# Two start-up weight loads move from SyncE's DMA queue to ScalarE's, in an attention plus FFN layer kernel

## The reference

```python
xn = _layernorm(x, axis=-1)
x = x + _L0_attn_ref(xn, Wq, Wk, Wv, Wg, Wo, Ws1, Ws2, bs2, g_norm_weight) \
      + _L0_ffn_ref(xn, gate_W_packed, gate_scales, up_W_packed, up_scales, down_W_packed, down_scales)
```

```python
q = (hs @ Wq.T).reshape(B, T, H, DK)
k = (hs @ Wk.T).reshape(B, T, H, DK)
v = (hs @ Wv.T).reshape(B, T, H, DV).transpose(0, 2, 1, 3)
g = (hs @ Wg.T).reshape(B, T, H, DV)
```

## Time and profile before

| what | value |
|---|---|
| median of 3 runs | 1081.25 us (1080.89 to 1081.56) |
| the profiled execution | 1081.48 us |
| its span | 1079.7 us |
| TensorE busy | 1067.8 us (99%) |
| VectorE busy | 916.1 us (85%) |
| ScalarE busy | 653.8 us (61%) |
| GpSimd busy | 420.4 us (39%) |

### The profile page before, as it was taken

How to read it: one execution, slowest core, us unless ns; L and a number is a source line. 1 busy time by engine, 2 the same in 40 slices (tenths; PEclk the granted TensorE clock), 3 DMA queues, 4 the chain that set the end, 5 groups by cost and what they waited for, 6 DMA issues and landing times.

```text
span 1079.7 us, 20531 instructions
## 1 busy us (share of the span) xinstructions
PE 1067.8 (99%) x7158; PEld 919.4 (85%) x7158; DVE 916.1 (85%) x1679; ACT 653.8 (61%) x2112; POOL 420.4 (39%) x309
## 2 busy tenths in 40 slices
PE   8999999999999999999999999999999999999999
PEld 6788888888888888888888888888888888888888
DVE  6998888888889888889878898889888889888886
ACT  5766665566655576555766556656565665656564
POOL 5353352434523354232643326343253432524332
PEclk9999999999999999999999999999999999999999
DMA  5020000200002000020000200002000010000001
GB/s 172 1 80 2 1 2 1 81 1 1 2 1 81 1 2 1 2 80 2 1 1 1 80 2 2 1 1 81 1 1 1 9 73 1 1 1 2 20 21 40
DMA packets 9558, 23.06 MB, mean 21 GB/s; under 512 B 880, under 2 KB 5872, under 8 KB 8560
## 3 DMA queue, kind: packets, MB, share of 16 engines
q1 hardware_dynamic: 9456, 21.76, 5.6%
HBM read 19.66 MB, written 2.10 MB: 20 GB/s over the span
## 4 chain that ended last, share of the span: by engine, by line
PE 93%; DVE 3%; ACT 1%; issue 1%; DMA 1%; SPq 0%; POOL 0%; DVEq 0%; POOLq 0%; ACTq 0%
PE bank L221 21%; PE bank L223 21%; PE bank L222 21%; PE bank L326 5%; PE bank L396 5%; PE bank L367 3%; PE bank L339 3%; PE bank L328 3%; PE bank L405 3%; PE bank L316 2%; PE bank L342 1%; PE bank L376 1%; PE bank L389 1%; PE bank L358 1%; PE bank L351 1%
## 5 line engine op out<-in xcount | busy, mean ns | idle before, releaser
L1458 POOL TENSOR_TENSOR inter_lo<-ffb,inter_hi 128x512 fp32r<-128x512 f32 x62 | 79.7, 1309 | 446.5 <-ACT inter_hi L811 446.5
L1449 POOL TENSOR_TENSOR qkT<-ra,xs 128x512 f32<-128x512 f32 x128 | 164.8, 1288 | 136.2 <-DVE xs L1121 114.4
L774 ACT ACTIVATE sm<-bank,mx 128x64 f32<-128x64 f32 x256 | 76.5, 325 | 145.3 <-DVE mx L1077 145.2
L1121 DVE TENSOR_TENSOR xs<-xs,rope 128x512 f32<-128x512 f32 x128 | 130.3, 1018 | 0.0
L755 ACT ACTIVATE xs<-bank 64x512 f32<-64x512 f32 x128 | 76.2, 595 | 79.3 <-PE bank L223 48.4
L1118 DVE TENSOR_TENSOR ra<-bank,rope 128x512 f32<-128x512 f32 x128 | 87.9, 687 | 35.2 <-ACT xs L756 33.4
L1066 DVE RECIPROCAL enzT<-enzT 128x256 f32<-128x256 f32 x64 | 111.6, 1744 | 0.0
L221 PE MATMUL bank<-xh,wgu_hi 128*128 128x512 f32 x256 | 105.3, 411 | 0.0
L221 PE MATMUL bank<-xh,wqk_hi 128*128 128x512 f32 x256 | 103.0, 402 | 0.8 <-DVE ffa L1102 0.8
L221 PE MATMUL bank<-wvg_hi,xh 128*128 128x512 f32 x256 | 100.8, 394 | 1.0 <-DVE xl L1177 1.0
L223 PE MATMUL bank<-xh,wgu_lo 128*128 128x512 f32 x256 | 101.0, 395 | 0.0
(11 more groups left out here) (173 smaller groups left out, 3057.0 us busy)
## 6 DMA issues: line engine op xcount, KB each, us to landing
raw<-in_w_qkvg SPq DMA_DIRECT2D x7, 1024.0 KB, 7.2
scaled<-in_w_scaled SPq DMA_DIRECT2D x8, 640.0 KB, 8.3
packed<-in_w_packed SPq DMA_DIRECT2D x8, 384.0 KB, 3.1
acc<-in_x SPq DMA_DIRECT2D x3, 512.0 KB, 9.6
out<-acc SPq DMA_DIRECT2D x3, 512.0 KB, 3.0
raw<-in_w_qkvg SPq DMA_DIRECT2D x2, 512.0 KB, 6.4
acc<-in_x SPq DMA_DIRECT2D x2, 256.0 KB, 3.0
ws_raw<-in_w_slot SPq DMA_DIRECT2D x8, 48.0 KB, 3.0
```

The costliest lines, as they stand in the source:

```text
L774: ins = act.activation(sm[:, c], src[:, c], ACT.Exp, bias=mx[:, g:g + 1], accum_out=ssum[:, g:g + 1])
L1121: dve.tensor_tensor(two(xs[i % 2][:, :]), two(xs[i % 2][:, :]), sin, ALU.mult).then_inc(sin_done, 1)
L1449: pool.tensor_tensor(qkT[:, i, :], ra[i % 2][:, :], xs[i % 2][:, :], ALU.add).then_inc(roped, 1)
L1458: pool.tensor_tensor(dst[1][e], ffb[e][:, :], dst[0][e].bitcast(F32), ALU.subtract).then_inc(inter_lo, 1)
```

## The change

Both weight loads are taken out of SyncE's program and put at the head of ScalarE's, ahead of its first wait. They write the same tiles and raise the same semaphores. SyncE's other loads move up by two places.

```diff
-            first = w_qkvg[0].rearrange("p (k n) -> p k n", k=KT)
             sp.dma_start(acc[:, 0:2, :], x_rows[:, 0:2, :]).then_inc(x_in[0], 16)
             sp.dma_start(acc[:, 2:NT, :], x_rows[:, 2:NT, :]).then_inc(x0_rest_in, 16)
-            sp.dma_start(raw_k[:, :, 512:1024], first[:, :, 512:1024]).then_inc(raw0_in, 16)
-            sp.dma_start(raw_k[:, :, 0:512], first[:, :, 0:512]).then_inc(raw_in, 16)
             load_x(1)
...
+            first = w_qkvg[0].rearrange("p (k n) -> p k n", k=KT)
+            act.dma_start(raw_k[:, :, 512:1024], first[:, :, 512:1024]).then_inc(raw0_in, 16)
+            act.dma_start(raw_k[:, :, 0:512], first[:, :, 0:512]).then_inc(raw_in, 16)
             act.wait_ge(raw0_in, 16)
```

## The result

The changed kernel took 1085.25 us in the median of 6 runs (1084.62 to 1085.69), the kernel before 1080.93 beside it (1080.51 to 1081.56): a ratio of 1.004, interval 1.0029 to 1.005. The forecast was 1081.4 with a range up to 1083.5, so it was wrong, and the time is near that of the third rival (1084.7), which had been given 0.06.

A forecast was written before the change was run, and what follows sets the result against it. TensorE, busy 1067.8 of 1079.7 us, was taken as the bound, so only the start could shift. The sum was 1081.48 + 0 + 0.24 = 1081.7 us, stated as 1081.4 for a median, range 1080.2 to 1083.5.

The forecast's parts named there:

- rival 3: TensorE's longer idle time before the transposes also lowers its clock: +1.5 us more, time 1084.7; chance 0.06.
- What bounds the start: TensorE's start is a chain from x, not the weights, without slack; any shift carries to the end unchanged.
- ScalarE's two issues cost nothing: Two issues ahead of ScalarE's table load, 1.3 us, are hidden because it waits until 7.65 us anyway: cost 0.
- net shift = d - 0.96: Late x delays TensorE, less its 0.96 us wait for batch pair 1: +0.24 us net.
- d: Delay of the second half of x of batch pair 0 from sharing the DMA engines with the weights: taken as 1.2 us.
- half of the bytes: Case where the weights take half of the DMA bytes from 2.5 us on, delaying x's second half by 1.5 us.
- the weights begin slowly: Case where the weights start at 107 GB/s for 0.75 us, then take half the rate: x's second half 1.0 us late.
- rival 2: DMA engines take packets in turn, x gets a third: its second half 2.95 us late, net +2.0, time 1083.2; chance 0.20.
- the hole: Low DMA rate after x's loads, 107 then 242 GB/s; earlier SyncE issues could fill it, landing later loads up to 0.85 us earlier.
- The bound that I set on a loss: Whole kernel: slower by over 2.2 us was given only 0.09, no change 0.90, faster 0.01.

The follow-up runs named there:

- 1 KB rows: Changed kernel with the weights loaded as four quarters in rows of 1 KB instead of 2 KB, 15 warm-up products: 1082.70 us against 1080.84 before.
- one queue: Kernel before, all loads on SyncE's queue, with x's second half issued behind the v/g weights instead of ahead: 1085.46 us against 1080.84.

## Why the prediction was wrong

**What bounds the start: right.** The chain from x's second half to the first projection has no slack, as read from the earlier trace rows. Everything on it moved by the same amount: statistics +2.73, normalised x +2.78 (6.86 to 9.64), transposes +2.78 (8.30 to 11.08). The shift also went to the end unchanged: +3.91 at 21.07 us, and +3.88 at the last group of output stores (1080.32 against 1076.44).

**ScalarE's two issues cost nothing: right.** 0.64 and 0.63 us, the table load at 2.12, and a wait of 3.18 us behind it.

**The rule "net shift = d - 0.96": right to 0.2 us.** With the clock up (27 warm-up products), the first projection moved from 10.50 to 13.20, d = 2.70, which gives 1.74; the transposes moved by 1.58. It needs the other loads to be in time: with 1 KB rows and 24 products, d is 1.02 and the transposes moved by 0.91 (17.16 to 18.07), because the q/k weights were late.

**The size of d: the first step that failed.** I took 1.2 us, between "half of the bytes" (1.5) and "the weights begin slowly" (1.0); it measured 2.7. The number is near that of rival 2, packets in turn (2.95), which was put at 0.26 together with rival 3 because no row showed two queues at once; "half of the bytes" was no better founded. But the nearness is luck, for the rows don't show what rival 2 describes. What they show is an order: x's second half waits for the weights that were issued ahead of it.

| kernel | weights issued ahead of x's second half | that half is used at, us |
|---|---|---|
| before | none | 4.46 |
| x on ScalarE, the rest held to 1.9 us | none | 4.45 |
| x on ScalarE, the rest held to 1.3 us | none (0.05 us behind it) | 4.57 |
| 1 KB rows (15, 21 and 24 products) | 256 KB | 5.21, 5.48, 5.48 |
| only the v/g half on ScalarE | 512 KB | 7.01 |
| changed (15, 27 and 21 products) | 512 KB | 7.19, 7.11, 7.30 |
| one queue | 512 KB | 7.33 |

(The first three have one block of statistics; the time is its start and half of its length.) One queue, on which nothing can be taken in turn, gives the same delay as two. By this order 2 x 524 - 60 = 988 KB have to be through, which at the 356 GB/s of the earlier trace rows is again d = 1.5. The rest comes from a lower rate (258, 306 and 302 GB/s from 2.5 to 5.5 us) and from the q/k half, which moved beside x's second half from 4.75 us on; how much each is worth isn't measured. Nor is the part of the packets' size, since the kernel with 1 KB rows has fewer bytes ahead as well. The Trainium skill, "DMA: Bandwidth & Descriptors", section "Queues, rings and completion order", says that each DMA engine takes whole packets in turn from the queues with work. The trace doesn't show that from 3.75 to 4.75 us, with 134 packets of weights to 33 of SyncE's queue; whether x's second half was ready to be taken then, it doesn't show either.

**The clock: the step that failed in weight.** Rival 3 got 0.06, as something that might come on top of rival 2. It came in seven of the eleven profiles after the change or of its variants, all of them with a first projection later than before, and in all six executions of the changed kernel. Here it cost 2.33 us at the transposes, more than the late x itself, and 1.5 by medians. I had priced it at 1.5 from the first slow stretch; the low level lasted longer, 6.8 us. Without it the late x costs 1.58 us at the transposes and 2.8 by medians, on either side of the 2.2 that count as a change; with it the kernel is clearly slower. That rival 3's time came so near is luck in part: it had a pause of 4 us, and it was 2.98.

**What the hole is worth: the price was fair, and the cause holds so far.** I put it at 0.85 us and to SyncE's issues. The rate from 3.75 to 4.5 us follows the moment at which the first load other than x of batch pair 0 was issued: 239 to 358 GB/s in the nine profiles where that was 0.80 to 1.30 us, and 107, 104 and 183 in the three where it was 1.79 to 1.89. Loads issued 0.5 us earlier brought 1.03 us at the transposes of batch pair 1. With the change the hole was filled too, but at the price of the rate before it, and behind a late x nothing waits for what it brings.

**The bound that I set on a loss was the real mistake.** I argued faster than 0.2% out of the question, rightly, and treated a loss as d - 0.96 with small chances beyond. A transfer on the path had no lead of its own once the second queue started at the same instant, and nothing in the rows bounded what it would lose.

**Slips in the sums, none of which decides.** Where two queues share by bytes or by packets, only the 464 KB of x that are left count, twice or three times: d is 1.3 instead of 1.5, and for rival 2 2.6 instead of 2.95. 1081.7 - 0.23 is 1081.5, not 1081.4, and rival 3 with a fifth of rival 2 is 0.10, not 0.09.

**What stays open.** What exactly makes the clock fall, the runs don't settle. It is a matter of chance as well as of the kernel. With a pause of 2.88 us or more before the transposes (2.98, 3.83, 2.88 and 3.13 in the profiles) it fell in 20 of 20 executions, with 2.61 before the projection in 7 of 9, with 2.19 in 5 of 10, with 0.97 in 3 of 10, in the kernel before (1.17) in 7 of 66, and with pauses of 0.19, 0.31, 0.32 and 1.14 us in 1 of 42. The pause itself varies from one execution to the next: the same 15 warm-up products took 4.99 to 6.18 us in the eight profiles that have them, since they came to full pace at different moments. So one profile shows what a fall looks like, but not how often it comes. Open too are how the engines choose between two queues, and what the hole from 4.5 to 5.5 us consists of (242 GB/s before, and 268 where the loads came earlier).

## What to carry to other kernels

Issuing a load on a second queue takes away the order that one queue gave for free. If an urgent load and a large one start together, what the urgent one issues behind the large one waits for it (here 0.75 to 1.0 us with 256 KB ahead and 2.6 to 2.9 with 512); give the urgent one a lead (here 0.5 us of a semaphore wait was enough), or leave both on one queue. And price a delay ahead of the first matmuls with the clock: 2.7 us of late data cost 1.6 at the transposes by themselves and 2.3 more through TensorE's pause. And read the clock of every execution, not only of the profiled one.

## What the runs showed of the hardware that was not expected

- The low level of TensorE's clock lasted 3.4 us in some kernels and 6.8 in others, and outlived the pause that went before it: in the changed kernel TensorE was at work from 11.08 us on, but reached full pace only at 17.6.
- Two queues with loads issued 0.5 us apart were served nearly in the order of issue, not packet for packet: with 512 KB of weights issued at 0.80 and x's second half at 1.28, ScalarE's queue moved 160 packets from 3.25 to 4.25 us and SyncE's 11.
- The same kernel kept TensorE's full clock in some executions and lost it in others (5 of 10 with 1 KB rows, 1.0 us apart; 7 of 66 before, about 2 us apart).
- A load can be hurt from either side: x by weights (7.19 instead of 4.46 us), or the weights by later, less urgent loads (9.66 instead of 7.65 us), each with the issue times nearly unchanged.
